# The causal mask of the row scores, written into PSUM by ScalarE instead of added by TensorE

## What is computed

```python
x = layernorm(x + time_and_channel_mix(x))   # linear recurrence over time, width 512
x = layernorm(x + soft_tree(x))              # 256 leaves, depth 8
x = layernorm(x + attention(x))              # 16 heads of 8, rotary, causal
x = layernorm(x + experts(x))                # top 2 of 16, and two shared ones
```

```python
scores = einsum('bthd,bshd->bhts', q, k) / sqrt(8) + causal   # -inf above the diagonal
weights = softmax(scores)
out = einsum('bhts,bshd->bthd', weights, v) @ Wo
```

## Time and profile before

| | us |
|---|---|
| median of 3 runs (1747.52 to 1748.81) | 1748.6 |
| the profiled execution's own time | 1748.68 |
| its span | 1746.5 |
| TensorE clock granted, mean of the span | 0.965 of full speed |

### The profile page before, as it was taken

One profiled execution on the slowest core, in us unless ns is written; L12 is line 12 of the kernel. 1 busy time (PEld: TensorE's weight loads), 2 busy tenths in 40 slices (PEclk: granted clock), 3 DMA queues, 4 the chain that ended last, 5 costly groups with the idle time before them and its releaser, 6 DMA issues.

```text
span 1746.5 us, 33903 instructions
## 1 busy us (share of the span) xinstructions
PE 1586.1 (91%) x12128; PEld 1089.7 (62%) x12205; DVE 1459.7 (84%) x3450; ACT 1004.7 (58%) x2014; POOL 911.6 (52%) x1121
## 2 busy tenths in 40 slices
...
DMA packets 66970, 53.36 MB, mean 31 GB/s; under 512 B 8370, under 2 KB 65522, under 8 KB 66802
## 3 DMA queue, kind: packets, MB, share of 16 engines
...
...
## 4 chain that ended last, share of the span: by engine, by line
PE 63%; DVE 20%; SPq 6%; ACT 5%; issue 4%; DMA 2%; POOL 1%; ACTq 0%; POOLq 0%; DVEq 0%; another core or an unknown queue 0%
PE bank L932 59%; DVE rmax L748 6%; SPq L313 5%; PE bank L928 4%; DMA kh<-part 2%; DVE inner L656 2%; DVE stats L647 2%; ACT prob L500 1%; DVE mixed L656 1%; DVE rmax L745 1%; DVE mv L652 1%; DVE xc L783 1%; ACT xbT L500 1%; ACT gT L500 0%; ACT part L500 0%
## 5 line engine op out<-in xcount | busy, mean ns | idle before, releaser
L500 ACT ACTIVATE prob<-bank 128x512 f32<-128x512 f32 x640 | 351.9, 601 | 170.1 <-PE bank L932 168.6
L748 DVE TENSOR_REDUCE rmax<-bank 128x1 f32<-128x512 f32 (+2 forms) x768 | 358.2, 504 | 49.8 <-PE bank L932 49.4
L446 POOL TENSOR_TENSOR prob<-xdT,spread 128x512 f32<-128x512 f32 x128 | 175.5, 1371 | 258.6 <-ACT spread L500 257.3
L932 PE MATMUL bank<-kh,qh 72*128 72x512 bf16 (+3 forms) x1024 | 252.5, 306 | 22.9 <-DVE rmax L748 9.9
L932 PE MATMUL bank<-wexpT,prob 128*128 128x128 f32 x2048 | 267.9, 276 | 3.1 <-issue 2.0
L932 PEld LDWEIGHTS bank<-wexpT,prob 128*128 128x128 f32 x2048 | 260.8, 192 | 11.4 <-issue 6.2
L932 PE MATMUL bank<-qh,kh 75*128 75x512 bf16 (+3 forms) x1024 | 242.8, 303 | 7.4 <-ACT prob L500 5.7
L695 DVE RECIPROCAL wkb<-wkb 128x512 f32<-128x512 f32 x64 | 213.7, 3340 | 0.0
L932 PE MATMUL bank<-maskb,identb 128*128 128x128 bf16 x1024 | 193.1, 222 | 0.0
L932 PE MATMUL bank<-maskTb,identb 128*128 128x128 bf16 x1024 | 191.2, 221 | 0.0
L500 ACT ACTIVATE spread<-bank 128x512 f32<-128x512 f32 x128 | 76.2, 596 | 185.5 <-PE bank L932 175.5
...
## 6 DMA issues: line engine op xcount, KB each, us to landing
...
```

What stands on the lines that cost most here:

```text
L446: raised(pool.tensor_tensor(ug[:, e % 4, :], xdT[:, :], spread[e // 2 % 2][:, :], ALU.mult), "ug_side")
L500: raised(act.activation(dst, src, func, **kw), signal)
L748: last = dve.tensor_reduce(rmax[:, j, h:h + 1], S[n % 2][:, col:col + (j + 1) * P], AX_X, ALU.max)
L932: return pe.matmul(out_, w, x, start=start, stop=stop, **kw)
```

## The change

It does four things.

1. ACT writes the mask into the bank (`row_mask`): one ACTIVATE with Identity for each unit copies `maskb` into the last 128 columns of the unit's piece, or of both its pieces at once. What PE waited for before a unit, ACT waits for now, and PE waits for ACT (`row_mask` n+1).
2. PE makes no mask product in the row stage. Each piece is two products with the same weights: the columns before the diagonal block, with the start flag, and the diagonal block, without it. A piece of tile 0 is one product. A sequence has 112 products for its rows, where it had 64 and 64 for the mask.
3. DVE reduces a unit of 384+128 columns with one instruction of four maxima over 128 columns each (into `rall`) where it had two. The three maxima of tile 2 are brought together in a new first step of `max_parts`, once for each half of the heads.
4. The order tables are written anew for POOL, ACT, DVE and PE. SP's is as it was. The tables begin at another point of the turn, so most of their lines differ without a step having moved.

The diff, with the tables cut to the lines around the end of the score stage:

```diff
--- before.py
+++ after.py
@@ -44,7 +44,7 @@
-    row_ps=UNITS, rowmax=UNITS, max_part=8, maxT_ps=2, maxT=2, max_in=32, score_ps=UNITS, prob=UNITS, pv=16, pvT=2, back_ps=2, pv_inv=2, att=2,
+    row_mask=UNITS, row_ps=UNITS, rowmax=UNITS, max_part=10, maxT_ps=2, maxT=2, max_in=32, score_ps=UNITS, prob=UNITS, pv=16, pvT=2, back_ps=2, pv_inv=2, att=2,
@@ -54,41 +54,44 @@
...
+        1:rwkv2 1:rwkv3 2:part_lo0 2:rope_sum1 2:rest1 0:root0 2:part_lo1 1:root2 0:x1_gain 4:root7 2:root4 3:root6 0:x1_bias 1:res 0:root1 1:cmr_sig
...
+        3:exp37 2:part_mid1 3:exp38 3:exp39 2:rmask0 0:norm0 2:rmask1 3:pvT_out1 1:norm2 3:attT_out 1:mix_before3 1:mix_before4 2:rmask2 2:rmask3
...
+        0:moments0 2:rope_mul3 1:x2 1:moments2 3:attend0 3:attend1 4:moments7 2:rowmax0 2:rowmax1 3:yc 1:mix3 1:mix4 3:moments6 2:rowmax2 2:rowmax3
...
+        3:weigh9 3:weigh10 3:score30 3:score31 3:weigh11 3:score32 1:weights 2:rope3 3:score33 3:back0 3:score34 3:score35 1:read_out0 1:read_out1
...
+        3:score36 3:score37 1:read_out2 1:read_out3 3:score38 3:score39 3:weigh12 3:weigh13 3:weigh14 3:weigh15 3:back1 3:attT 1:xn2T 2:row0 2:row1
...
@@ -182,7 +185,9 @@
         bias_part = [part[0][i][0:1, :] for i in range(PARTS)]
         qh, kh = sb("qh", [KALL, NH, T], BF16), sb("kh", [KALL, NH, T], BF16)
         vaug = sb("vaug", [P, J * NQ * V_STEP])
-        rmax, max_rest = sb("rmax", [P, J, NH]), sb("max_rest", [P, J, NH])
+        rall, max_rest = sb("rall", [P, PARTS + J, NH]), sb("max_rest", [P, J, NH])
+        rmax = rall[:, PARTS:PARTS + J, :]
+        PLACE = (0, 1, 3, 2)
         gate_cols = sb("gate_cols", [P, (J - 1) * PARTS * NH + P], BF16)
         gate_part = gate_cols[:, 0:J * PARTS * NH].rearrange("p (j i h) -> p j i h", j=J, i=PARTS)
         max_cols = [sb(f"max_cols{z}", [P, (J - 1) * HALF_MAX + P], BF16) for z in range(2)]
@@ -585,6 +590,28 @@
                     freed = [("pv", 16 * b + 4 * (n // 10 - 1) + (4 if n % 5 == 4 else 3 if n % 5 % 2 else 1))]
                 move(b, prob[:, slot_of(n), :], S[n % 2], "score_ps", "prob", n + 1, func=ACT.Exp, freed=freed, scale=float(DH) ** -0.5)
 
+            def row_mask(b, n):
+
+                if b == 0 and n == 0:
+                    act.wait_ge(setup["ident"], 4)
+                if n >= 2 and n != FREED_FOR_MAXIMA + 2:
+                    until(act, b, "rowmax", n - 1)
+                elif n >= 2:
+                    until(act, b, "maxT", 1)
+                else:
+                    until(act, b - 1, "prob", UNITS - 1 + n)
+                spans = [(col + j * P, col + (j + 1) * P) for _, j, col in pieces(n)]
+                bank_ = S[n % 2]
+                if len(spans) == 1:
+                    last = act.activation(bank_[:, spans[0][0]:spans[0][1]], maskb[:, :], ACT.Identity)
+                elif spans[0][1] == spans[1][0]:
+                    both = bank_[:, spans[0][0]:spans[1][1]].rearrange("p (z s) -> p z s", z=2)
+                    last = act.activation(both, maskb[:, :].rearrange("p (o s) -> p o s", o=1).broadcast_to([P, 2, P]), ACT.Identity)
+                else:
+                    both = bank_.rearrange("p (z s) -> p z s", z=2)[:, :, P:2 * P]
+                    last = act.activation(both, maskb[:, :].rearrange("p (o s) -> p o s", o=1).broadcast_to([P, 2, P]), ACT.Identity)
+                raised(last, "row_mask")
+
             def weighed(b, k):
                 move(b, pvT[:, :], O, "pv", "pvT", (12, 16)[k], freed=[("back_ps", 2 * b + 1)] if k else [])
 
@@ -599,7 +626,7 @@
                 "xcT_out": lambda b: move(b, xcT[:, :], A1, "xcT_ps", "xcT"),
                 "values": take_values, "vaug": place_values, **each("part_hi", 2, first_part), **each("part_mid", 2, second_part),
                 **each("maxT_out", 2, lambda b, z: move(b, maxT[:, :], (S[0], G)[z][0:HALF_MAX, :], "maxT_ps", "maxT", z + 1, freed=[("max_in", 16 * (2 * b + z))])),
-                **each("exp", UNITS, score), **each("pvT_out", 2, weighed),
+                **each("rmask", UNITS, row_mask), **each("exp", UNITS, score), **each("pvT_out", 2, weighed),
                 "attT_out": lambda b: move(b, attT[:, :], G, "attT_ps", "attT"),
                 "xdT_out": lambda b: move(b, xdT[:, :], G, "xdT_ps", "xdT"),
                 "route_exp": lambda b: move(b, lex[:, :, :], lsh[:, :, :], "route", "lexp", 3, func=ACT.Exp),
@@ -740,19 +767,22 @@
 
             def row_maxima(b, n):
                 until(dve, b, "row_ps", n + 1)
+                h = pieces(n)[0][0]
                 if n % 5 == 4:
-                    h = 2 * (n // 5)
-                    last = dve.tensor_reduce(rmax[:, 1, h:h + 2], S[n % 2].rearrange("p (h s) -> p h s", h=2), AX_X, ALU.max)
+                    last = dve.tensor_reduce(rmax[:, PLACE[1], h:h + 2], S[n % 2].rearrange("p (h s) -> p h s", h=2), AX_X, ALU.max)
+                elif n % 5 % 2:
+                    last = dve.tensor_reduce(rall[:, 0:PARTS + 1, h], S[n % 2].rearrange("p (z s) -> p z s", z=J), AX_X, ALU.max)
                 else:
-                    for h, j, col in pieces(n):
-                        last = dve.tensor_reduce(rmax[:, j, h:h + 1], S[n % 2][:, col:col + (j + 1) * P], AX_X, ALU.max)
+                    last = dve.tensor_reduce(rmax[:, PLACE[3], h:h + 1], S[n % 2], AX_X, ALU.max)
                 raised(last, "rowmax")
 
             def max_parts(b, z):
 
                 heads = slice(z * NH // 2, (z + 1) * NH // 2)
-                to, of, left, done = max_part[z], rmax[:, :, heads], max_rest[:, :, heads], 4 * z
+                to, of, left, done = max_part[z], rmax[:, :, heads], max_rest[:, :, heads], 5 * z + 1
                 until(dve, b, "rowmax", (z + 1) * UNITS // 2)
+                raised(dve.tensor_reduce(rmax[:, PLACE[2], heads], rall[:, 0:PARTS, heads].rearrange("p z h -> p h z"), AX_X, ALU.max), "max_part")
+                until(dve, b, "max_part", done)
                 if z == 0:
                     until(dve, b - 1, "maxT_ps")
                 raised(dve.tensor_scalar(to[:, :, 0, :], of, -1.0, None, ALU.mult), "max_part")
@@ -1050,33 +1080,27 @@
 
             def row_scores(b, n):
 
-                if b == 0 and n == 0:
-                    pe.wait_ge(setup["ident"], 4)
                 if n == 0:
                     until(pe, b, "heads_low")
                 if n == UNITS // 2:
                     until(pe, b, "heads_high")
-                if n == FREED_FOR_MAXIMA + 2:
-                    until(pe, b, "maxT", 1)
-                elif n >= 2:
-                    until(pe, b, "rowmax", n - 1)
-                elif n == 0:
-                    until(pe, b - 1, "prob")
+                until(pe, b, "row_mask", n + 1)
                 for h, j, col in pieces(n):
-                    to = S[n % 2][:, col:col + (j + 1) * P]
-                    mm(to, qh[0:KROWS, h, j * P:(j + 1) * P], kh[0:KROWS, h, 0:(j + 1) * P], True, False, skip_group_check=True)
-                    last = mm(to[:, j * P:(j + 1) * P], identb[:, :], maskb[:, :], False, True, skip_group_check=True)
+                    to, q = S[n % 2][:, col:col + (j + 1) * P], qh[0:KROWS, h, j * P:(j + 1) * P]
+                    if j:
+                        mm(to[:, 0:j * P], q, kh[0:KROWS, h, 0:j * P], True, True, skip_group_check=True)
+                    last = mm(to[:, j * P:(j + 1) * P], q, kh[0:KROWS, h, j * P:(j + 1) * P], False, True, skip_group_check=True)
                 raised(last, "row_ps")
 
             def turn_maxima(b, z):
-                until(pe, b, "max_part", 4 * (z + 1))
+                until(pe, b, "max_part", 5 * (z + 1))
                 if z:
                     until(pe, b - 1, "ug")
                     until(pe, b - 1, "spread_out")
                 else:
                     until(pe, b, "rowmax", FREED_FOR_MAXIMA + 1)
                 for j in range(J):
-                    last = mm((S[0], G)[z][:, j * P:(j + 1) * P], max_cols[z][:, j * HALF_MAX:j * HALF_MAX + P], identb[:, :])
+                    last = mm((S[0], G)[z][:, j * P:(j + 1) * P], max_cols[z][:, PLACE[j] * HALF_MAX:PLACE[j] * HALF_MAX + P], identb[:, :])
                 raised(last, "maxT_ps")
 
             def scores(b, n):
```

56 lines of the change are left out of this document (27 added, 29 removed).

## The result

The changed kernel takes 1768.25 us (median, 1767.57 to 1769.01), the kernel before 1748.6. The ratio is 1.0111, 95% interval [1.0093, 1.0129], so it is slower by 19.6 us, where the prediction had 9.4. The side is right, the time lies in the range, and the size is only half of what was measured. The profiled execution has a span of 1765.4 us against 1746.5.

A forecast was written before the change was run, and what follows sets the result against it. The prediction took PE and DVE to bound the kernel together, in a 97.40 us period. Stretches of 85.5 + 12.5 = 98.0 us add 0.6 a period, 15 times, 9 us: forecast 1758 us, range 1729 to 1786.

The forecast's parts named there:

- Part 1: PE's 64 mask products leave each period, at 0.06 us each: 3.8 us less PE work a period.
- Passage: DVE from the end of the last inverse to the next first row maximum: 12.5 us, before 9.7.
- the two chains: In the passage: kh's transfer, first maximum at 12.4 us, and norm2 on ACT with xn2T, first maximum at 12.7.
- Part 2: DVE's maxima: 1.0 us saved a period by single reduces, 0.5 given back in max_parts, 0.5 us gain kept.
- Part 3: ACT's mask writes: 0.28 us for one block, 0.4 for two, some 14 us on ACT; idle time left unchanged.
- rival (b): Mask writes queue on ACT, holding PE outside the passage (sign: above 2 us a period); 1782 us, chance 0.2.
- Part 4: The new order's effect on DVE's period, cut into two stretches: 85.5 + 12.5 = 98.0 us against 97.4.
- first stretch: DVE from the first row maximum to the end of the last inverse: 87.7 us before, 85.5 forecast.
- Sum: Over the whole kernel, 15 periods of 0.6 us more each make 9 us; forecast 1758 us.
- Rival (a): The passage closes earlier and PE's relief counts: second stretch 11.0, 1.2 us less a period, 1731 us, chance 0.33.
- second stretch: The passage on DVE, last inverse to next first row maximum: 12.5 us forecast; below 11.9 would decide for Rival (a).

The follow-up runs named there:

- POOL's short instruction: The changed kernel with POOL's gated inputs cut to 16 of 512 columns: 1749.8 us; the same cut in the new order without any row mask: 1725.5 us.

## Why the prediction was right and wrong

- **Part 1.** Right: PE's busy time fell by 3.6 us a period, 3.8 forecast.
- **Passage.** Right: 12.72 us against 12.5 forecast, PE idle for 1.8 us against "about 2". kh's first issue was 4.5 us behind the inverse, 4.4 forecast. Of the two chains that the prediction let end together, the one on ACT came last and kh did not; its last members were pvT_out1, back1 and the division, since norm2 was done 0.26 us before xn2T.
- **Part 2.** Right in its parts: the reduce with four results takes 681 ns (683 taken), the small one adds 0.2 us (0.25 taken). Alone, it is worth nothing.
- **Part 3, the write's own price.** Right: 278 and 384 ns, 0.28 and 0.4 taken. What the Trainium skill (ScalarE: Activation LUTs, Rules for kernel authors) gives, 0.41 and 0.51, was too high here. Its 0.3 us are stated for an ACTIVATE whose bias is read from memory as a column, and the mask write has none; the prediction left this condition out. **Its place in the loop** was costed at nothing ("I leave its idle time unchanged"). That was wrong. PE waits 2.8 us a period for mask writes outside the passage, 1.0 of them at route_exp. That is rival (b)'s mechanism, at the place that it named and above its sign of 2 us. What it costs depends on what else the order does: 8.6 us beside the stalls, 24 us with POOL's short instruction, about half of it in periods in which the clock fell. Of the three falls in the changed kernel two begin where PE waits 1.0 us for a mask write (659.0 and 1054.8) and one in the passage (249.4); that these waits caused them is likely and not shown, since the same wait in other periods brings no fall.
- **Part 4, first stretch: the step that failed.** It took 87.7 less the work that left, with each remaining instruction at its old duration. But a new order also decides what runs beside what. kvsum0 and tree3 stood still for 2.1 us a period behind POOL, and the experiment that takes this away takes 18.5 of 19.6 us away. DVE's busy time, which was to fall by 0.5 us a period, rose by 0.9. That the stretch came out only 0.45 us above the forecast 85.5 was luck: waits of 1.9 us that the sum had kept went at the same time, two omissions of opposite sign. With neither stalls nor masks the stretch is 83.8.
- **Sum.** Forecast 15 x 0.6 = 9. In place of 0.6 a period stands 1.27; 0.45 of the difference is from the first stretch and 0.22 from the passage. And three periods have 1.5 more for the clock, a term that the sum did not have. The start is 0.2 later and the end 1.3 shorter, as assumed about nothing.
- **Rival (a)**, 1731 us, did not come. Its gain is not shown for a kernel with mask writes: with the stalls away that one is level with the kernel before (1749.8). Without masks and stalls the new order reaches 1725.5, but there it has neither the mask products nor the mask writes. The second stretch does not decide it, as the prediction had it: it is 12.57 in that kernel, well above 11.9, and the time is in the first.
